# Linear attention and a routed FFN on one core: other orders at the ends of the batch pipeline, and one halving less per batch

## The reference

```python
# 1: linear cross-attention, 8 heads of 64, over channels-first maps (128 x 1024)
q = Wq @ layernorm(x); k = Wk @ ctx; v = Wv @ ctx
q = softmax(q, over the 64 rows of a head) * 64**-0.5
k = softmax(k, over the 1024 positions)
context = k @ v.T                       # per head, 64 x 64
o = Wo @ (context.T @ q) + bo
o = o / max(l2norm(o, over the 128 channels), 1e-12) * g * sqrt(128)
x = x + tanh(g_xattn) * o
# 2: 64 experts of rank 16, 16 of them chosen per row (2048 rows in all)
xf = layernorm(x)
scores = xf @ Wr.T
gates = softmax(top_k(scores, 16)) scattered into 64
h = xf @ A (1024 values per row); h = h * gates
x = x + tanh(g_ffn) * (h @ B) * 2.0
```

## Time and profile before

| what | value |
|---|---|
| median of 3 runs | 907.29 us (906.74 to 909.43) |
| profiled execution | 906.83 us |
| its span in the trace | 905.1 us |
| TensorE busy | 882.1 us, 97% of the span |
| VectorE, ScalarE, GpSimd busy | 82%, 75%, 60% |
| attention bodies, from context to context | 31.96, 31.89, 31.92, 31.40, then 31.0 each, 31.74 for b=14, 34.24 for b=15 |
| first context | 38.55 us |
| FFN's first product | 520.08 us |

### The profile page before, as it was taken

One profiled execution on the slowest core, in us unless ns is written; L12 is line 12 of the kernel. 1 busy time (PEld: TensorE's weight loads), 2 busy tenths in 40 slices (PEclk: granted clock), 3 DMA queues, 4 the chain that ended last, 5 costly groups with the idle time before them and its releaser, 6 DMA issues.

```text
span 905.1 us, 15780 instructions
## 1 busy us (share of the span) xinstructions
PE 882.1 (97%) x4604; PEld 742.8 (82%) x4604; DVE 742.8 (82%) x1515; ACT 678.4 (75%) x1392; POOL 543.8 (60%) x374
## 2 busy tenths in 40 slices
PE   6899999999999999999999899999999999999998
PEld 4677877888888888888877788889899989999996
DVE  5899899899889989998897878887778778877642
ACT  4877887788778777877886758588888878888731
POOL 3697797799899989988899956232222212222100
PEclk9999999999999999999999999999999999999999
DMA  4434645654674557354632894212221212211001
GB/s 162 164 102 156 211 139 162 213 177 166 185 239 153 180 164 227 122 164 162 192 103 94 293 347 147 70 70 71 71 71 71 71 59 75 76 65 52 24 24 47
DMA packets 46846, 120.88 MB, mean 134 GB/s; under 512 B 5712, under 2 KB 21072, under 8 KB 46800
## 3 DMA queue, kind: packets, MB, share of 16 engines
q1 hardware_dynamic: 41040, 99.37, 32.9%
q0 software_dynamic: 5472, 20.45, 7.1%
q10 hardware_dynamic: 288, 0.52, 0.2%
HBM read 87.82 MB, written 32.51 MB: 133 GB/s over the span
## 4 chain that ended last, share of the span: by engine, by line
PE 67%; DVE 10%; POOL 9%; issue 7%; ACT 5%; DMA 2%; DVEq 0%; POOLq 0%; ACTq 0%
PE ps L61 20%; PE ps L62 19%; PE ps L63 19%; PE ps L1579 4%; PE ps L1570 3%; ACT h_raw L835 3%; PE ps L1560 2%; POOL qe L490 1%; DMA aT_hi<-in_AT 1%; POOL xn_lo L456 1%; POOL ctxT_lo L449 1%; POOL qhalf L475 1%; POOL x L570 1%; POOL qe L485 1%; POOL qT_lo L495 1%
## 5 line engine op out<-in xcount | busy, mean ns | idle before, releaser
L567 POOL TENSOR_TENSOR rb<-u_in,rb 128x1024 f32<-128x1024 f32 x14 | 33.7, 2405 | 216.0 <-DVE rb L1060 216.0
L61 PE MATMUL ps<-aT_hi,yT_hi 128*128 128x448 f32 (+2 forms) x360 | 119.4, 332 | 2.0 <-DVE hg L1220 1.4
L62 PE MATMUL ps<-aT_hi,yT_lo 128*128 128x448 f32 (+2 forms) x360 | 118.1, 328 | 0.0
L63 PE MATMUL ps<-aT_lo,yT_hi 128*128 128x448 f32 (+2 forms) x360 | 118.0, 328 | 0.0
L835 ACT ACTIVATE h_raw<-hg 32x256 f32<-32x256 f32 x248 | 103.1, 416 | 17.3 <-DVE hg L1253 14.5
L835 ACT ACTIVATE y_raw<-u_in 32x256 f32<-32x256 f32 x216 | 89.5, 415 | 7.0 <-DVE u_in L1236 4.6
L61 PE MATMUL ps<-bT_hi,hT_hi 128*128 128x512 f32 x240 | 93.7, 390 | 0.0
L62 PE MATMUL ps<-bT_hi,hT_lo 128*128 128x512 f32 x240 | 93.5, 390 | 0.0
L63 PE MATMUL ps<-bT_lo,hT_hi 128*128 128x512 f32 x240 | 93.4, 389 | 0.0
L490 POOL TENSOR_TENSOR qe<-qe,qrec 128x1024 f32<-128x1024 f32 x48 | 91.3, 1902 | 1.4 <-DVE qrec L1082 1.4
L731 ACT ACTIVATE qe<-ps 128x1024 f32<-128x1024 f32 x48 | 49.1, 1024 | 42.1 <-PE ps L1560 42.1
(11 more groups left out here) (186 smaller groups left out, 2671.5 us busy)
## 6 DMA issues: line engine op xcount, KB each, us to landing
x_in<-in_x SPq DMA_DIRECT2D x16, 512.0 KB, 4.3
ctx_in<-in_ctx SPq DMA_DIRECT2D x16, 512.0 KB, 5.6
ctxT_in<-in_ctxT SPq DMA_DIRECT2D x16, 512.0 KB, 4.3
ctxT_hi<-in_ctxT POOLq DMA_DIRECT2D x16, 512.0 KB, 3.7
turn_q_scratch<-qe SPq DMA_DIRECT2D x16, 512.0 KB, 2.6
qe<-turn_q_scratch SPq DMA_DIRECT2D x64, 128.0 KB, 2.9
u_scratch<-osb SPq DMA_DIRECT2D x16, 512.0 KB, 2.9
x<-in_x SPq DMA_DIRECT2D x15, 512.0 KB, 4.0
```

What stands on the lines that cost most here:

```text
L61: nc.tensor.matmul(psum, whi, mhi, start=start, stop=False)
L62: nc.tensor.matmul(psum, wlo, mhi, start=False, stop=False)
L63: return nc.tensor.matmul(psum, whi, mlo, start=False, stop=stop)
```

## The change

Seven edits, on all engines but SyncE:
1. `sum_q(b, 2)` reads the 1024 columns of the exponentials itself, as `sum_q(b, 3)` does; `halve(b, 2)` is gone (16 GpSimd instructions).
2. ScalarE: `out_o(b-1, 0)` moves from before `exp_q(b, 2)` to behind `hi_k(b, 3)`, in every batch; `scale_first(1)` in the last body likewise.
3. Batch 0: `fold_weights` goes ahead on TensorE; `mm_q(0, 3)` stands right behind `tr_k(0, 2)`, and `mm_k(1, 0)` behind `tr_k(0, 3)`; ScalarE, VectorE and GpSimd follow that order.
4. Batch 1 on VectorE (`second`): `sum_q(0, 2)`, `max_q(1, 0)`, `lo_kc(0)`, `max_k(1, 1)` come before `turn_k`, `stats`, `std` and `sum_q(0, 3)`.
5. Batch 14 on VectorE: `early_guess` comes behind `lo_kc`.
6. Last head (batch 15): VectorE sums piece 1 before `krec` and piece 2 behind `max_q(15, 3)`, and does `stats2_sums(0, 0)` and `std2` last; on GpSimd `spread_first(1)` comes behind the weights' transfers `hi_a(3..7)` and `normalise(15, 1)`, and `add_first(1)` moves into body 16 behind `normalise(15, 2)` and `normalise(15, 3)`.
7. FFN: `sum_u(7)` goes behind `up(5, 1)` (so i = 1 is written out on TensorE, and the loop holds i = 2 alone); VectorE does `stats2_sums(3)` before `lo_moved_h(1)` in batch 1.

In the rows below, a name `out<-in` gives what an instruction writes and reads; L-numbers of the changed kernel are shifted by up to 6. VectorE, end of batch 0 and start of batch 1, before: `qsum` is `sum_q`, `qtop` is `max_q` of piece 3, `ekT_lo` is `lo_k`, `ek<-ek` is `turn_k`, `bn` is `stats`.

The diff, cut to its core (a moved line stands as - and +):

```diff
 # GpSimd
-                if p > 1 or started(b):
-                    pool.wait_ge(q_sum, 4 * b + p - 1)
+                if started(b):
+                    pool.wait_ge(q_sum, 4 * b + p - 2)
...
                 if tail and not head:
+                    add_first(1)
                     lo_moved_q(b - 1)
...
-                if head and not ahead:
-                    spread_first(1)
                 if ahead:
                     lo_xn(b + 1, 0)
-                if head:
                     normalise(b, 1)
-                if head and not ahead:
+                elif head:
                     for t in range(3, DC):
                         hi_a(t)
-                if head:
-                    halve(b, 2)
+                    normalise(b, 1)
+                    spread_first(1)
...
-                if head and not ahead:
-                    add_first(1)
 # ScalarE
+                if head:
+                    exp_q(b, 2)
+                    hi_k(b, 2)
+                if ahead and not started(b):
+                    hi_k(b, 3)
+                    hi_xn(b + 1, 0)
+                    exp_q(b, 3)
+                    exp_k(b + 1, 0)
+                elif ahead:
+                    hi_xn(b + 1, 0)
+                    exp_k(b + 1, 0)
+                if head and started(b):
+                    hi_k(b, 3)
+                if tail and head:
+                    out_o(b - 1, 0, early)
                 if head and not ahead:
                     scale_first(1)
-                if tail and head:
-                    out_o(b - 1, 0, early)
-                if head:
-                    exp_q(b, 2)
...
 # VectorE
-                if p == 3:
-                    dve.wait_ge(q_exp, 8 * b + 8)
-                    whole = qe[:, 3, :].rearrange("p (h d) -> p h d", d=DH)
+                if p >= 2:
+                    dve.wait_ge(q_exp, 8 * b + 2 * p + 2)
+                    whole = qe[:, p, :].rearrange("p (h d) -> p h d", d=DH)
...
+                elif last:
+                    lo_k(b, 3)
+                    max_q(b, 3)
+                    sum_q(b, 2)
+                    stats2_sums(0, 0)
+                    std2(0, range(NCH + 1))
...
+                if norms:
+                    stats2_sums(b + 2, (j + 3) % SLOTS)
+                if first:
                     lo_moved_h(1)
                 if norms:
-                    stats2(b + 2, (j + 3) % SLOTS)
+                    std2(b + 2, range(NCH + 1))
 # TensorE
                 if head:
                     tr_k(b, 2, next(turn))
+                if head and not started(b):
+                    mm_q(b, 3)
...
+                if head and started(b):
                     mm_q(b, 3)
+                elif head:
+                    mm_k(b + 1, 0)
...
-                late = isinstance(i, int) and b in (1, 2, 4)
+                late = isinstance(i, int) and b in (1, 2, 4, 5)
...
-            with pe.Fori(1, NB // SLOTS - 1) as i:
+            for j in range(SLOTS):
+                ffn_body(1, j)
+            with pe.Fori(2, NB // SLOTS - 1) as i:
```

More of the change, by code:

```diff
@@ L582, in body @@
                     normalise(b - 1, 2)
+                if head and not started(b):
+                    hi_c(b)
                 if head:
                     halve(b, 0)
+                if head and not started(b):
+                    lo_c(b)
                 if tail:
@@ L870, in body @@
             def body(b, head, tail, ahead, early=False):
-                if tail:
+                if tail and not (isinstance(b, int) and b == 1):
                     exp_q(b - 1, 3)
@@ L896, in body @@
                     exp_k(b, 1)
+                    if not started(b):
+                        act.wait_ge(fold_done, 1)
+                        for par in range(2):
+                            nc.scalar.activation(wvo[0][:, :, par * P:par * P + P],
+                                                 psX[:, par, :].rearrange("p (j o) -> p j o", o=P),
+                                                 ACT.Copy, scale=DH ** -0.5).then_inc(fold_hi, 1)
                 if tail:
@@ L1321, in body @@
                     std(b + 1, range(5))
-                if tail:
+                second = isinstance(b, int) and b == 1
+                if tail and head:
                     sum_q(b - 1, 2)
+                if second:
+                    max_q(b, 0)
+                    lo_kc(b - 1)
+                    max_k(b, 1)
                 if head and turned(b):
@@ L1327, in body @@
                     stats(b + 1)
-                if ahead and started(b):
                     std(b + 1, range(3))
@@ L1331, in body @@
                     sum_q(b - 1, 3)
-                if head and started(b):
+                if head and started(b) and not second:
                     max_q(b, 0)
+                if tail and not second:
+                    lo_kc(b - 1)
                 if norms:
                     early_guess()
-                if tail:
-                    lo_kc(b - 1)
-                if head and started(b):
+                if head and started(b) and not second:
                     max_k(b, 1)
@@ L1383, in body @@
                     spread(2, rb, n_newton, 4 * NEWTON)
+                if last:
+                    sum_q(b, 1)
                 if head:
@@ L1386, in body @@
                     nc.vector.reciprocal(krec[:, :], ksum[:, :]).then_inc(k_rec, 1)
+                if ahead and started(b):
+                    max_k(b + 1, 0)
+                if head:
+                    lo_k(b, 2)
                 if last:
@@ L1723, in body @@
                     shift_q(b, 0)
+                    if not started(b):
+                        fold_weights()
                 if tail:
@@ L1740, in body @@
                     shift_q(b, 1)
-                    if not started(b):
-                        fold_weights()
                 if tail and not (head and turned(b)):
@@ L1756, in body @@
                     output(b - 1, 0, range(CH - 1, CH))
-                if ahead:
+                if ahead and started(b):
                     mm_k(b + 1, 0)
```

40 lines of the change are left out of this document (11 added, 29 removed).

## The result

The changed kernel takes 911.43 us (median of 5 runs, 910.5 to 912.69); the kernel before took 907.29 (905.6 to 909.43) beside it. The ratio is 1.005, interval 1.0031 to 1.0069: slower by half a per cent. The forecast was 906.8, range 903.0 to 910.0. The profiled execution has a span of 908.9 us, 3.8 more than before, so the two traces hold the whole difference.

What follows compares the result with a forecast made beforehand. TensorE, busy 97% of the span, was taken as the bound, so only its idle time could be won. Start -1.0, tail +2.35 and FFN -1.4 gave -0.05 on 906.83: 906.8 us, range 903.0 to 910.0.

Steps and rivals of the forecast that it cites:

- The first context: Batch 0: context(0) at about 35.4 us, 3.2 us earlier than 38.55.
- the shorter early bodies: Batches 1 to 3: moving the scaled result on ScalarE gives 0.4 us each, -1.2 in all, bounds 0 and -1.5.
- the last head's -1.8: Batch 15: both waits on ekT_lo and their restarts go, context(15) at 509.05 instead of 510.88.
- the FFN's -1.4: FFN batch 5: the 1.51 us wait for part goes, 0.3 comes back later; -1.4, bounds 0 and -1.7.
- the wider sum at 0: Batches 5 to 13: VectorE's sum of piece 2, 0.53 us longer a batch, is covered by slack; 0.
- The start was lent: Batches 0 and 1: the 3.2 us gained are given back, max_q(1,1) at 52.0 to 52.7; net +0.2.
- 0.15 us for a restart: Last head: estimated TensorE restart cost after each of the two ekT_lo waits, counted in the -1.8.
- the tail's term, +2.35: Seam before the FFN: u_done, x_second's load, add_first(1), lo_y(0) put up(0,0) at 523.0, +2.9; net +2.35.
- the block behind it was put at -0.6: up(0,0): aT_hi's transfers issued earlier, so the 0.40 us weight wait and its restart go; -0.6.
- my rival with a chance of 0.11 and a price of 3: Seam: TensorE's clock falls to 1.2 GHz in the pause of about 4.5 us; +3, 909.8, chance 0.11.
- +4.3: Seam: upper bound of the tail's term, if x_second's load took 2 us longer beside the eight weight transfers.
- VectorE has slack: Batch 14: reason given for edit 5's worth of 0, along with the moved Newton guess being short.

Runs made afterwards that it cites:

- scaled_back: Changed kernel with edit 2 undone: out_o(b-1,0) and scale_first(1) stand before exp_q(b,2) again; 914.67 us, ratio 1.0088.
- piece_two_only: Kernel before with edit 1 alone (piece 2 summed whole, no halving); 909.1 us, ratio 1.0011.
- own_place: Changed kernel with x_second in the halvings' unused memory, so its load waits for sum_q(15,1) instead of u_done 2; 906.91 us, ratio 0.9995.
- pool_order_back: Changed kernel with GpSimd's seam order as before: spread_first(1), normalise(15,1), five weight transfers, add_first(1), all in the last head; 911.41 us, ratio 1.0043.
- all_four: Changed kernel with batch 1 reordered, x_second moved and loaded ahead of the weights, GpSimd's last head reordered, sum_u(8) behind up(6,1); 899.84 us, ratio 0.9919.
- last_batch_back: Changed kernel with edit 6 undone on VectorE, ScalarE and GpSimd, piece 2 still summed whole; 906.04 us, ratio 0.9984.
- spread_ahead: Changed kernel with spread_first(1) ahead of the five weight transfers and normalise(15,1); 909.43 us, ratio 1.002.
- all_three: Changed kernel with start_filled, own_place, and GpSimd's last head as normalise(15,1), weight transfers, spread_first(1), add_first(1); 907.83 us, ratio 1.0004.
- pause_filled_more: Changed kernel with 34 unused identity matmuls on TensorE before up(0,0), filling its pause; 910.35 us, ratio 1.0037.
- start_filled: Changed kernel with sum_q(0,3) and turn_k(1) ahead of max_q(1,0) on VectorE in batch 1; 909.63 us, ratio 1.0027.
- start_four_back: Changed kernel with edit 4 undone: VectorE's batch 1 order as before, edit 3 kept; 911.57 us.
- pause_filled: Changed kernel with 24 unused identity matmuls on TensorE before up(0,0), in its pause; 912.51 us.
- ffn_back: Changed kernel with edit 7 undone on TensorE and VectorE; 915.24 us, ratio 1.0081.

## Why the prediction was wrong

**Right by its own steps.** The first context (35.4 forecast, 35.71), the shorter early bodies (0.4 each forecast, 0.5 measured, and edit 2's, by `scaled_back`), the last head's -1.8, the FFN's -1.4 (-1.56; 0.54 came back in batch 6, where I gave 0.3), the wider sum at 0 (`piece_two_only`). The start was lent, as argued: `max_q(1,1)` at 52.84 where I had 52.0 to 52.7. Two slips of my working are small: 31.4 + 0.6 + 3.6 is 35.6, not 35.4, and my own marks make the pause 5.0 us long, not 4.5. And 0.15 us for a restart was an estimate without a row: behind a wait the second matmul starts 0.33 us after the first instead of 0.23 (510.88 and 511.21 in the trace of before), 0.10 more. It was luck that the rest of the sum held: the start gave 0.6 us less than forecast and body 14 with its neighbours 0.45 more.

**The step that failed is the tail's term, +2.35.** Its chain was the right one, link by link, and `own_place` shows it. Its size was not: in the time of the kernel before (0.89 us, the gain of the stretches ahead, added to the marks after) `up(0,0)` comes at 525.4 instead of 523.0, and the block behind it was put at -0.6 and is +0.94. That makes +6.2, and the 3.9 us between are the whole miss. Of them:
- 0.7 us: `u_done` 2 at 515.4 instead of 514.7, small delays of GpSimd's instructions.
- 1.7 us: the load took 6.2 us, not 4.5. I called 4.5 "at most", which is true of that one trace (4.4 from issue to landing), but used it for a load issued behind the five weight transfers where it had been issued ahead of them. Over all traces that difference is a clear one, though no run changed it alone. The load took 4.0 to 4.4 us in the three in which it went out ahead of the first weight transfer (by 0.5 us before, 1.8 in `pool_order_back`, 4.1 in `all_four`), 7.1 to 8.1 when it went out within 0.3 us behind it (`last_batch_back`, `piece_two_only`, `spread_ahead`), 10.5 and 12.1 when 1.6 and 2.0 us behind (`own_place`, `all_three`). With the changed kernel's order at the seam, 7.0 us behind it, it took 6.1 to 7.8 in eight traces, with pauses of TensorE to match: 6.61 us here, 8.19 and 8.28 where the load took 7.7 and 7.8. So the 4.5 was a figure for another place in the line of transfers, and a single sample of it.
- 1.5 us: the clock, 1.7 at full price (`pause_filled_more`). That was my rival with a chance of 0.11 and a price of 3.

**The bounds were combined wrongly.** The load being 2 us late was inside the forecast (+4.3), the clock was a rival beside it. But in all seven traces whose pause before `up(0,0)` was 3.9 us or more, the clock fell in that pause or right behind it. The two belong together, and together they give 910.4 (906.8 + 1.95 for the load + 1.7 for the clock), above the range. The rival should have hung on the size of the pause that I had just worked out myself, twice as long as any in the trace of before.

**Batch 1.** I counted the give-back there as queue time alone. The clock fell there too, to 0.55 behind waits of 1.15 and 1.91 us, and in other traces with the same start body 1 took from 35.40 to 36.95 us. Against `start_filled`, TensorE is idle in body 1 for 2.2 us longer and busy for 0.9 us longer, so the clock's own part there is about 0.9 us (an estimate from these two windows); no run took it away by itself.

**Body 14.** I gave edit 5 nothing for "VectorE has slack"; it gave 0.5 us. The slack is an average over the body: `lo_kc` stood behind the guess, and TensorE's `fold` waits for it.

The Trainium skill ("TensorE: Matmul & The Clock Gate", What's actually happening) states that TensorE gets half the clock once it has idled, and the full one once it has been busy again. The trace agrees: behind the pause the same matmuls start 0.37 us apart, and later 0.20.

## What to carry to other kernels

Before moving an instruction that frees memory for a load, follow who waits for the load's memory in turn, and issue the load ahead of the bulk transfers: here it took 4.0 to 4.4 us ahead of them, and 6.1 to 12.1 behind. Look at the issue times in the trace for this, not at the programs: two engines issue them, and a load that went out 0.06 us behind the first of them took 3.2 us longer (`piece_two_only`). A pause of TensorE costs its length and, if the clock falls, half-speed matmuls behind it (1.7 us here), so work lent from one stage to the next has to be paid back without leaving one; look for the hole in the engine that lends (here 2.70 us of VectorE) and put the deferred work there.

## What the runs showed of the hardware

Whether the clock fell did not follow from the length of the last pause alone. It did not fall behind 2.28 us (`last_batch_back`) or 2.66 (`piece_two_only`), both at the seam; it did behind 2.94 (`start_four_back`), behind 1.15 and 1.91 in batch 1, behind 2.60 that followed 24 unbroken matmuls (`pause_filled`), and behind 1.63 in FFN batch 5 of `ffn_back`, though the same wait, 1.51 us long there, left it at 1.00 in the kernel before. At the start of the kernel it fell behind 1.26 and 1.37 in the changed kernel, not behind 2.16 and 1.38 in the kernel before, nor behind 1.43 and 1.37 in `start_filled`. A wait that is harmless in one trace is not so in the next.

The same holds from one execution of a kernel to another, and a single trace hides it. The kernel before was timed 80 times beside the experiments. In 36 of these executions its mean granted clock was 1.000, with a median of 906.39 us; in 38 it was 0.998 or less, with a median of 908.37. The trace of before, at 1.000, has no fall, and that of `own_place`, with one, is at 0.997. So the kernel whose trace shows no fall seems to have one or more in about half of its executions, which are 2 us longer; no trace of such an execution tells where. The changed kernel's five executions were at 0.992 to 0.994, the four of `all_four` at 0.997 to 1.000.
